# Second attention: projections and value products of a stride in a row, its transposes behind them

## What is computed

```
q, k, v = x @ Wq.T, x @ Wk.T, x @ Wv.T          # 32 heads of 64
q, k = apply_rope(q, k)
local heads (30), for each block of 128 queries from `start`:
    keys from max(0, start - 64) to start + 128
    a = softmax(where(query >= key, q k^T / 8, -inf));  out = a @ v
global heads (2): the same with all keys up to the query
y = out @ Wo.T + bo
```

## Time and profile before

| | us |
|---|---|
| runs shown | 3080.47, 3091.6, 3095.89; median 3091.6 |
| the profiled execution | 3078.77 |
| its span, first to last instruction | 3077.0 |
| TensorE busy (matmuls) | 2951.5 (96%) |
| VectorE, ScalarE, GpSimd busy | 2102.8 (68%), 1852.0 (60%), 1019.7 (33%) |
| mean granted TensorE clock | 0.992 |
| second attention, from 1635.40 to the end | 1441.60, TensorE busy 1410.35 |

### The profile page before, as it was taken

The page is one execution under the profiler, slowest core; times in us unless marked ns, Lnnn a source line. Parts: engine busy times, 40 slices in busy tenths (PEclk is TensorE's granted clock), DMA queues, the critical chain, the costliest instruction groups (busy, mean ns, idle before and its releaser), DMA issues. The chain is left out here.

```text
span 3077.0 us, 66534 instructions
## 1 busy us (share of the span) xinstructions
PE 2951.5 (96%) x23638; PEld 2231.5 (73%) x23638; DVE 2102.8 (68%) x5890; ACT 1852.0 (60%) x4638; POOL 1019.7 (33%) x1627
## 2 busy tenths in 40 slices
PE   7999999999999999998898999999999999999998
PEld 5888888864444444444787888788887888788886
DVE  5666666689999999994765565655556555665556
ACT  4666666658877777775445555455554555545553
POOL 0000000001100000001005666576665766667663
PEclk9999999999999999999999999999999999999999
DMA  4111111231332323301415545454453555355442
GB/s 154 49 49 49 49 49 42 63 70 33 83 46 57 50 36 66 50 6 38 151 45 142 115 112 116 111 139 108 112 130 99 133 118 114 81 127 123 111 111 72
DMA packets 360644, 262.23 MB, mean 85 GB/s; under 512 B 213116, under 2 KB 295676, under 8 KB 360188
## 3 DMA queue, kind: packets, MB, share of 16 engines
q1 hardware_dynamic: 360316, 257.98, 34.6%
HBM read 100.85 MB, written 44.04 MB: 47 GB/s over the span
## 5 line engine op out<-in xcount | busy, mean ns | idle before, releaser
L1007 ACT ACTIVATE a_pt<-ps 128x512 f32<-128x512 f32 x1024 | 556.1, 595 | 170.6 <-PE ps L1043 169.6
L176 DVE TENSOR_REDUCE mx<-ps 128x2 f32<-128x1024 f32 x512 | 622.0, 1224 | 50.0 <-PE ps L167 34.9
L1847 ACT ACTIVATE b_pp<-b_pp,b_nm 128x192 f32<-128x192 f32 (+2 forms) x1024 | 472.8, 463 | 279.3 <-DVE b_nm L2025 209.4
L1817 POOL TENSOR_SCALAR b_pp<-b_pp,b_rc 128x192 f32<-128x192 f32 x960 | 389.3, 428 | 283.6 <-DVE b_rc L2034 283.6
L797 DVE SCALAR_TENSOR_TENSOR f_yac<-ps,f_cw,f_yac 128x128 f32<-128x128 f32 x992 | 278.1, 344 | 125.3 <-PE ps L596 123.0
L2046 DVE COPY b_pt<-ps 128x320 f32<-128x320 f32 (+2 forms) x336 | 166.3, 509 | 276.7 <-PE ps L1941 263.1
L596 PEld LDWEIGHTS ps<-w,f_sq 128*128 128x128 f32 x2048 | 265.2, 191 | 26.5 <-issue 6.0
L2025 DVE CUSTOM_DVE_ANT_0 b_pp<-ps,b_mk 128x192 f32<-128x192 f32 x480 | 170.0, 354 | 158.0 <-PE ps L1919 158.0
L596 PE MATMUL ps<-w,f_sq 128*128 128x128 f32 x2048 | 270.2, 275 | 0.3
L1976 PE MATMUL ps<-b_wo,b_oT 128*128 128x256 f32 x1024 | 241.2, 379 | 0.0
L1056 PE MATMUL ps<-a_pt,a_v 128*32 128x256 f32 x3072 | 239.3, 391 | 0.0
(11 more groups left out here) (291 smaller groups left out, 7817.8 us busy)
## 6 DMA issues: line engine op xcount, KB each, us to landing
b_rt<-b_qf SPq DMA_DIRECT2D x1024, 64.0 KB, 2.0
qk_parts<-f_aa SPq DMA_DIRECT2D x32, 512.0 KB, 2.7
b_vs<-b_vv SPq DMA_DIRECT2D x120, 128.0 KB, 2.9
b_vb<-b_vv SPq DMA_DIRECT2D x120, 128.0 KB, 3.0
b_vs<-b_vv SPq DMA_DIRECT2D x120, 112.0 KB, 2.8
v_rows<-f_va_ SPq DMA_DIRECT2D x16, 512.0 KB, 2.8
rl<-in_W1vT SPq DMA_DIRECT2D x32, 256.0 KB, 3.3
b_wo<-in_W1oT SPq DMA_DIRECT2D x16, 512.0 KB, 3.8
```

What stands on the lines that cost most here:

```text
L176: e.tensor_reduce(M["mx"][kh % 3][:, :, jt, h], P.pair(s), AX.X, ALU.max, negate=True).then_inc(P.free_sem(s), 1)
L1007: e.activation(pt[(4 * i + 2 * j + a) % 12][:, :], P.ap((*s, a)), ACT.Exp).then_inc(P.free_sem((*s, a)), 1)
L1817: m = e.tensor_scalar(x, x, r[:, 2 * u + h:2 * u + h + 1], 1.0, ALU.mult, ALU.mult)
L1847: e.activation(x, x, ACT.Exp, bias=nm[n % 4][:, c:c + 1], scale=-1.0, accum_out=sm[n % 4][:, c:c + 1]).then_inc(exp_done, 1)
```

## The change

```diff
@@ -1498,18 +1498,12 @@
         evacs = [("evac", x[1]) for x in out if x[0] == "fourth"]
         out += exps[:3]
         exps = exps[3:]
-        for u in range(max(len(slots), len(turned))):
-            if u < len(slots):
-                out += slots[u]
-            if exps:
-                out.append(exps.pop(0))
-            if evacs and (u == 2 or len(slots) < 3):
-                out += evacs
-                evacs = []
-            if u < len(turned):
-                out.append(turned[u])
-        out += evacs
-        return out
+        if len(slots) < 4:
+            for x in slots:
+                out += x
+            return out + exps + evacs + turned
+        out += slots[0] + exps + slots[1] + slots[2] + evacs + slots[3]
+        return out + turned
```

## The result

| | before | changed |
|---|---|---|
| median of 9 runs, us | 3081.06 (3077.82 to 3095.89) | 3102.45 (3100.59 to 3105.84) |
| span of the profiled execution | 3077.0 | 3098.8 |
| second attention, first scores to the end | 1441.6 | 1462.6 |
| TensorE busy | 2951.5 | 2974.0 |

The ratio is 1.0065, 95% interval 1.0053 to 1.0078: slower, by about 21 us. Of the 21.8 us between the two spans, 21.0 lie in the second attention, and 0.8 in a later start of it.

What follows compares the result with a forecast made beforehand. TensorE's own stream, busy 229.60 of 229.60 us, was taken as the bound. Terms of 25 + 0.5 + 0 + 0 gave about +25 us on 3087, the mean of four executions: 3112 us, range 3098 to 3126.

Steps and rivals of the forecast that it cites:

- The main term: In 109 local strides, block 3 waits for block 0's bank: 0.23 us each, 25 us in all, bounds 16 and 34.
- The edges: Changes between kinds of matmul on TensorE: 0 us, with ±0.02 us a stride, ±2 us, as bounds.
- The Trainium skill's figure: 50 to 100 ns for a sequencer to read a semaphore; its lower end would make the sum some 7 us smaller.
- The strides without an output product: Seven first local strides: three gain 0.5 us, one loses about 1, three between 0 and +0.3; together 0, bounds −4 and +3.
- The three whole-row strides: Fourteen transposes behind the output product get one bank wait, about 0.2 us each: +0.5 us.
- Rival B: In steady strides the second rope product waits for its earlier DMA, holding VectorE's add and copy; 3140 to 3180 us, chance 0.10.
- the 1.1 us of cover: In a plain stride the rope ends 1.1 us before the output's add on VectorE begins, so a wait there is covered.
- Rival C: Twelve transposes together drop TensorE's clock to 1.2 GHz for one block a stride: +36 us, 3148 us; chance 0.03.
- A: Block 3's bank is free in time or the wait is hidden: no slower, 3078 to 3096 us; chance 0.16.
- D: The change doesn't reach TensorE's order, or shifted banks avoid the wait: same time, 3080 to 3096 us; chance 0.03.
- The sum: All terms over the whole kernel: 25 + 0.5 + 0 + 0, about +25 us; 3104 us on the profiled execution's basis.
- The predicted signs of the profile: Gaps before blocks 3 and 2, some 100 listed waits for VectorE's copy, plain stride 10.66 us, first strides' rope waits gone.

Runs made afterwards that it cites:

- e4: The changed kernel with the copies of blocks 0 and 2 on ScalarE, 1 and 3 on VectorE; plain stride 10.572 us, span 3092.7 us.
- e5: The changed kernel with block 0 left behind the first projection, blocks 1 to 3 behind the output product; plain stride 10.567 us, ratio to before 1.0033.
- e1_bank0: The changed kernel with block 0 of local strides in bank 0, not banks 4 to 6; median 3076.93 us against 3083.84 before, ratio 0.9977.
- e6_bank0_qf3: e1_bank0 with three qf buffers in place of two; second attention 1435.9 us, ratio to before 0.999.
- e7_whole_as_before: The changed kernel with strides 38, 76 and 114 (whole-row transposes) ordered as before; 9.81 us each, second attention 1464.6 us.
- the first experiments: Follow-up runs, each an edit of the changed kernel; the text does not say which of them are meant, so no single time applies.

## Why the prediction was right

- **The main term** was forecast at 0.23 us × 109 = 25 us. The transposes of a plain stride lost 0.215, and the stride as a whole 0.20. The mechanism is the one forecast: block 3 waits for block 0's copy, at T+1.17 where 1.18 was worked out, and 1.20 with the longer spacing where 1.21 was; block 2 waits for the output product's bank. Giving block 0 another bank took both waits away, and two banks made the stride 0.95 us longer than before. The prediction calls block 0's copy the main term and has block 2's 0.13 as a part of the 0.23. It is the larger part: with the copy early enough (e4) or block 0 in its old place (e5), a stride is still 0.13 us longer than before, from the output product's bank.
- **The edges.** I took 0 ± 0.02 us a stride. In the changed kernel everything in a plain stride but its transposes is 0.013 us shorter than before, 1.4 us over 109 strides and inside my bounds; the wait that came out at 0.215 and not 0.23 is another 1.6. e1_bank0 is shorter by a further 0.010 us, in the steps inside its projections, though its matmuls stand in the same order; no run shows why.
- **The Trainium skill's figure** for reading a semaphore (Advanced Engine Details and Errata, Network/Comms) would have lowered the sum by 7 us at its lower end; from the end of a copy to the weight load these runs show 0.12 us, so the row of the kernel before (0.11) was the better guide.
- **The strides without an output product** came to −0.3 us in all, where 0 was forecast: three gained 0.49 to 0.51, one lost 0.92, three lie between +0.04 and +0.14. The split is as forecast; that the sum came so near is in part luck, as it moves by 0.4 us between executions of the same code. What holds them (SP's DMAs) is shown by e6_bank0_qf3.
- **The three whole-row strides** went the other way: −0.4 us each for +0.2. The step that failed is "behind the output product they get one bank wait of the same kind, about 0.2 each", as the only effect of the move. No such wait came: the fourteen transposes take 1.93 us from first start to last end, as before (1994.51, ahead of the scores of 1996.37).

```profile
1994.51 1.93 PE L1925 MATMUL ps<-ident,b_pp 128*128 128x128 f32 x14
```

  What came in its place is e7_whole_as_before's 0.4 us. Moved behind the ropes, VectorE's four copies hide behind the scores that follow. Before, two of them stood ahead of the second rope on VectorE, and the scores waited for the rope's bank. I had looked at what the moved copies cost and not at what they had held up.
- **Rival B** (the rope's DMA holds VectorE, and the copies behind it) is real in strides 1, 3, 5 and 7, and of the 109 strides in stride 143 alone, where no value product separates the projections. In the changed kernel the second rope of stride 143 waits 1.66 us for the DMA, and block 2 then waits for the output's add:

```profile
3035.67 0.69 DVE L1991 TENSOR_TENSOR b_qf<-ps,xt 128x512 f32<-128x512 f32 x1 [1.66 <-DMA b_rt<-b_qf]
```

```profile
3037.44 0.30 PE L1933 MATMUL ps<-ident,b_pp 128*128 128x128 f32 x1 [1.01 <-DVE b_acc L2051]
```

  It cost 0.46 us there, 0.2 of them the common bank wait. In one plain stride, 19, the rope waited 1.08 us for the DMA; that stride took 10.63 us like its neighbours, so the 1.1 us of cover that the prediction worked out held.
- **Rival C** (the clock) did not appear: 1.00 in the plain stretch with twelve transposes in a row. The Trainium skill's sentence on transposes (TensorE: Matmul & The Clock Gate, Part 4), that they do not count as busy in the same way, made no difference here: rows of 1.4 us between other matmuls left the clock at 1.00. Rivals A and D fell with the stride of 10.64.
- **The sum** on the profiled execution was 3104 and came out at 3098.8 of span, some 3101 as a time. The forecast of 3112 lies 10 us over the median: 4 us are the sum, and 6 us the base. I put it on the mean of four executions, 3087; the median of before is 3081 over nine runs. The predicted signs of the profile held but for two. Some 100 listed waits of L1939 for the copy were to show up; there are seven, and those in other strides. And the larger gap between starts is the one before block 2, not the one before block 3.

## What to carry to other kernels

Work put together in a row meets its own buffers: count how many steps apart a bank comes round, and compare that with the read-out plus the hand-over (here 0.31 + 0.49 + 0.12 us behind the start of a block's last transpose, against the 0.76 us until the fourth block is due), and do so for every step in the turn, the output product too: its bank alone costs 0.13 us a stride here. If the gap is short, put other work between, or take an idle bank for one of them, before giving the order up. And on an engine that is busy all the time, measure a stall by the starts of its instructions; neither its busy share nor its list of waits has to show it.

## What the runs showed of the hardware that was not expected

The kernel before took 3076.1 to 3105.0 us in the 29 runs beside the first experiments, and the spread is not in the stage that was changed: in nine kernels' profiles the second attention began between 1635 and 1648 us, while the 104 plain strides of the kernel before lie between 10.43 and 10.44 us. The windows show where. Before:

```profile
660.00:680.00 20.00, 17.65 (x89) 12.18 (x87) 15.98 (x28) 3.55 (x6) 0.53 (x4) 1.00 0.01 2
680.00:700.00 20.00, 17.91 (x126) 7.18 (x130) 14.32 (x13) 13.69 (x26) 0.00 (x0) 0.74 0.60 133
700.00:720.00 20.00, 18.71 (x173) 7.88 (x165) 19.48 (x20) 15.63 (x29) 0.00 (x0) 1.00 0.01 2
```

e6_bank0_qf3, with the same code there:

```profile
660.00:680.00 20.00, 17.97 (x90) 12.37 (x89) 16.31 (x29) 3.36 (x6) 0.53 (x4) 1.00 0.01 2
680.00:700.00 20.00, 17.66 (x94) 6.43 (x94) 11.13 (x10) 11.30 (x21) 0.00 (x0) 0.53 0.60 134
700.00:720.00 20.00, 19.67 (x133) 7.05 (x130) 16.14 (x17) 11.92 (x23) 0.00 (x0) 0.70 0.01 2
```

Where one stage ends and the next begins, after a stretch in which TensorE was busy 17.6 to 18.0 of 20 us, part of the time goes by at the lower clock of 1.2 GHz. In the one run TensorE is back at full clock by 700 us, in the other not before 720, and 32 and 40 fewer matmuls start in these two windows (94 for 126, 133 for 173). Why it takes longer in some runs was not tried. For a difference of 0.2% on this kernel it means that the stage's own length from its first scores says more than a single time does: 1436.4 against 1441.6 us is clear beside the 0.5 us between e1_bank0 and e6_bank0_qf3, and the times took 12 runs against 29 to say so.
